# Nine one-unit slots for x, with joint loads in even periods and joint stores in odd ones, in a two-stage depthwise convolution

## The reference, cut to what matters

```python
def _L0_conv_ref(x, w1, w3, w5, alpha):      # depthwise, "same" padding
    return alpha[0]*x + alpha[1]*dw(x, w1) + alpha[2]*dw(x, w3) + alpha[3]*dw(x, w5)

def _L1_conv_ref(x, w, b):                   # one 3 x 3 kernel for all channels
    return conv3x3(x, w) + b

def _gn(v, G=32, eps=1e-05):                 # 32 groups of 3 channels
    ...
    return (g - mean) / sqrt(var + eps)

x = x + _L0_conv_ref(_gn(x), w1, w3, w5, alpha)
x = x + _L1_conv_ref(_gn(x), w, b)
```

## Time and profile before

| | |
|---|---|
| median of 3 runs | 429.32 us (427.31 to 429.94) |
| the profiled execution, its own time | 432.64 us |
| its span (first to last instruction) | 430.8 us |
| mean granted TensorE clock | 0.903 of full speed |
| busy PE, DVE, ACT, POOL | 318.5, 318.1, 304.1, 262.3 us |
| HBM read and written | 41.10 and 27.48 MB |

### The profile page before, as it was taken

How to read it: one execution, slowest core, us unless ns; L and a number is a source line. 1 busy time by engine, 2 the same in 40 slices (tenths; PEclk the granted TensorE clock), 3 DMA queues, 4 the chain that set the end, 5 groups by cost and what they waited for, 6 DMA issues and landing times.

```text
span 430.8 us, 12547 instructions
## 1 busy us (share of the span) xinstructions
PE 318.5 (74%) x5206; PEld 276.8 (64%) x5206; DVE 318.1 (74%) x688; ACT 304.1 (71%) x372; POOL 262.3 (61%) x206
## 2 busy tenths in 40 slices
PE   2491586754986998679894998499848989898440
PEld 2361273643986798459883897389836989897220
DVE  7861899971886998399929994889649996779620
ACT  1407257089999699939995899759993999977320
POOL 6405055058788578827885588738882788865601
PEclk9997596995999899969996999889998999999685
DMA  6689488201687769676986788676868514731965
GB/s 151 169 174 204 129 188 169 73 3 41 159 200 164 199 177 210 158 189 202 199 194 171 198 184 202 161 214 173 189 163 223 145 41 118 201 97 28 264 173 146
DMA packets 112829, 69.40 MB, mean 161 GB/s; under 512 B 4540, under 2 KB 109892, under 8 KB 112772
## 3 DMA queue, kind: packets, MB, share of 16 engines
q1 hardware_dynamic: 106088, 65.31, 60.5%
q10 hardware_dynamic: 6684, 3.29, 3.3%
HBM read 41.10 MB, written 27.48 MB: 159 GB/s over the span
## 4 chain that ended last, share of the span: by engine, by line
DVE 33%; DMA 21%; SPq 13%; ACT 13%; PE 9%; issue 4%; ACTq 2%; POOL 2%; POOLq 0%; DVEq 0%
DVE xt L697 15%; DVE stats L641 13%; DMA xt<-in_x_dram 10%; PE ps L377 8%; DMA edge_scratch<-gnX 6%; ACT gn_f L551 5%; SPq L236 5%; ACT gnX L552 4%; ACT cross L561 3%; SPq L216 3%; DMA edge_scratch<-gnY 2%; SPq L250 2%; POOL gnX L864 1%; SPq L263 1%; ACTq L244 1%
## 5 line engine op out<-in xcount | busy, mean ns | idle before, releaser
L377 PE MATMUL ps<-gnX,band 64*64 64x512 f16 x2880 | 181.6, 397 | 29.9 <-DVE xt L697 18.1
L377 PEld LDWEIGHTS ps<-gnX,band 64*64 64x64 f16 x2880 | 161.1, 188 | 46.6 <-issue 40.2
L697 DVE SCALAR_TENSOR_TENSOR xt<-ps,unscale,xt 128x512 f32<-128x512 f32 (+1 forms) x194 | 143.8, 747 | 22.9 <-PE ps L377 20.1
L641 DVE BATCH_NORM_STATS2 stats<-xt 128x6 f32<-128x384 f32 x256 | 120.9, 546 | 45.6 <-DMA xt<-in_x_dram 44.9
L377 PE MATMUL ps<-gnY,band 64*64 64x512 f16 x1728 | 116.8, 414 | 33.7 <-DVE xt L697 33.7
L864 POOL TENSOR_TENSOR gnX<-gn_f,gnX 128x768 f16<-128x768 f32 x60 | 92.7, 1545 | 60.7 <-ACT gnX L552 60.7
L377 PEld LDWEIGHTS ps<-gnY,band 64*64 64x64 f16 x1728 | 97.9, 190 | 49.1 <-ACT gnY L552 23.0
L551 ACT ACTIVATE gn_f<-xt,g_add,g_mul 128x768 f32<-128x768 f32 x120 | 122.1, 1017 | 4.9 <-DVE g_add L681 4.3
L864 POOL TENSOR_TENSOR gnY<-gn_f,gnY 128x768 f16<-128x768 f32 x60 | 92.7, 1545 | 31.0 <-ACT gnY L552 31.0
L561 ACT ACTIVATE cross<-ps,unscale 64x512 f32<-64x512 f32 x94 | 64.2, 683 | 51.0 <-PE ps L377 49.4
L873 POOL TENSOR_TENSOR xt<-xt,cross 128x512 f32<-128x512 f32 x47 | 61.7, 1315 | 57.3 <-ACT cross L561 57.2
(11 more groups left out here) (78 smaller groups left out, 97.9 us busy)
## 6 DMA issues: line engine op xcount, KB each, us to landing
out_dram<-xt SPq DMA_DIRECT2D x56, 384.0 KB, 4.8
xt<-in_x_dram SPq DMA_DIRECT2D x48, 384.0 KB, 6.4
band<-diag_scratch SPq DMA_DIRECT2D x48, 160.0 KB, 3.0
haloX<-edge_scratch SPq DMA_DIRECT2D x32, 123.4 KB
xt<-in_x_dram SPq DMA_DIRECT2D x20, 192.0 KB, 4.3
xt<-in_x_dram ACTq DMA_DIRECT2D x12, 192.0 KB, 6.0
out_dram<-xt SPq DMA_DIRECT2D x12, 192.0 KB, 4.0
haloX<-edge_scratch SPq DMA_DIRECT2D x32, 61.7 KB
```

Source lines behind the costliest of these rows:

```text
L377: mm = nc.tensor.matmul(ps[to, c, half, :], weights(rows, half), moving(rows, half), start=first, stop=last)
L641: st = nc.vector.bn_stats(stats[:, q_of(at, i) % 2, at, b, e, :], flat[:, SUB * e:SUB * (e + 1)])
L697: ev = nc.vector.scalar_tensor_tensor(out=here, in0=ps[frm, c, half, :].rearrange("h (b w) -> h b w", b=NB), scalar=unscale[rows, at:at + ...
```

## The change

The nine slots of `xt` hold one unit each (unit n in slot n % 9), and the two groups of a unit come from the two halves of the channels (unit n has channels 3n and 48 + 3n onwards). `PRE` = 4 units are loaded as before; the loads of units 4 and 5 stay in SP's period 1, and units j + 4 and j + 5 are loaded in even period j (2 to 10). Stores: unit 0 alone in period 3, then units j - 4 and j - 3 in odd period j (5 to 15), then units 13, 14 and 15 one by one. A pair whose slots lie side by side is one DMA per batch and half (384 KB); units 8 and 9 (slots 8 and 0) are loaded by two (192 KB each). Loads of a batch wait for the stores of that batch alone. To make room, `cross` has two buffers in turn in place of three, and `halo_wX` overlaps its blocks (pitch 66 in place of 128 columns). SP's order of border rows, bands and bulk within a period is as before.

```diff
-    NX = 4
+    NX = 9
+    PRE = 4
...
-        halo_w = [sb("halo_wX", [P, NU * CG, 2, R], fp16), sb("halo_wY", [P, 2, R], fp16)]
+        halo_w = [sb("halo_wX", [P, NU * CG * (R + FAR[0]) + R - FAR[0]], fp16), sb("halo_wY", [P, 2, R], fp16)]
...
-        xt = sb("xt", [P, NX, NB, 2, CG, 2, W])
+        xt = sb("xt", [P, NB, NX, CG, 2, W])
...
-        cross = sb("cross", [P, NCROSS, NB, W])
+        cross = sb("cross", [P, 2, NB, W])
...
         def first_channel(i, g):
-            return 4 * CG * (i // 2) + 2 * CG * g + CG * (i % 2)
+            return C // 2 * g + CG * i
...
+        def rows_of(n, g, b, units):
+
+            at = n % NX
+            return xt[HALVES[g], b, at:at + units, :, :, :].rearrange("p u c e w -> p (u c e) w")
+
+        def joint(n):
+
+            return n % NX + 1 < NX
...
+        def load(eng, n, b, units, done):
             for g in range(2):
...
+                eng.dma_start(rows_of(n, g, b, units), images(x, n, g, b, units)).then_inc(done, 16)
+
+        def store(eng, n, b, units):
             for g in range(2):
...
+                eng.dma_start(images(out, n, g, b, units), rows_of(n, g, b, units)).then_inc(stored[b], 16)
...
+            def stores_in(j):
+
+                if j < LAG + 1:
+                    return None
+                if j == LAG + 1 or j >= NU:
+                    return j - LAG - 1, 1
+                return (j - LAG - 2, 2) if j % 2 else None
+
+            def loads_in(j):
+
+                if j == 1:
+                    return PRE
+                return j + PRE if j % 2 == 0 and 2 <= j < NU - PRE else None
...
             def in_and_out(j, batches):
 
-                m = (j + 3) // 2 if j % 2 else j // 2 - LAG
                 for b in batches:
-                    if j % 2 and 2 <= m < NU // 2:
-                        if m >= NX:
-                            sp.wait_ge(stored[m % NX], 128 * (m // NX))
-                        load_pair(sp, m, b)
-                    elif j % 2 == 0 and m >= 0:
-                        unit_ready(2 * m + 1)
-                        store_pair(sp, m, b)
-                    elif j == PERIODS - 1:
-                        unit_ready(LAST - 1)
-                        store_unit(sp, LAST - 1, b)
+                    if stores_in(j) is not None:
+                        n, units = stores_in(j)
+                        unit_ready(n + units - 1)
+                        store(sp, n, b, units)
+                    n = loads_in(j)
+                    if n is not None:
+                        if n + 1 >= NX:
+                            sp.wait_ge(stored[b], 32 * stores_until(n + 1 - NX))
+                        if joint(n):
+                            load(sp, n, b, 2, x_in[n // 2 % 2])
+                        else:
+                            for k in range(n, n + 2):
+                                load(sp, k, b, 1, x_in[n // 2 % 2])
...
             def cross_over(i, c):
...
-                if i >= 1:
-                    act.wait_ge(cross_added, NCROSS * (i - 1) + min(c, NCROSS - 1) + 1)
+                k = crosses_before(i, c)
+                if k >= 2:
+                    act.wait_ge(cross_added, k - 1)
...
-            nc.vector.memset(halo_w[X][:, :, :, :], 0.0).then_inc(halo_w_zero, 1)
+            nc.vector.memset(halo_w[X][:, :], 0.0).then_inc(halo_w_zero, 1)
```

More of the change, by code:

```diff
@@ L133, in preact_conv_stack @@
         x_unit_in = [sem(f"x_unit_in{n}") for n in range(1, 4)]
-        x_in = [sem(f"x_in{r}") for r in range(NX)]
+        x_in = [sem(f"x_in{r}") for r in range(2)]
         band_in = [sem(f"band_in{p}") for p in range(2)]
-        stored = [sem(f"stored{r}") for r in range(NX)]
+        stored = [sem(f"stored{b}") for b in range(NB)]
         edges_landed = [sem(f"edges_landed{s}") for s in "XY"]
@@ L193, in crossed_to, with crosses_before @@
             return sum(crossed(n, c) for n in range(i + 1) for c in range(CG))
+        def crosses_before(i, c):
+            return crossed_to(i - 1) + sum(crossed(i, k) for k in range(c))
         def halo_landed(n):
@@ L239, in edges_in, with images, loaded @@
                        .then_inc(halo_in[s][p], 16)
-        def load_unit(eng, n, b, done):
+        def images(t, n, g, b, units):
+            c = first_channel(n, g)
+            return t[b, c:c + units * CG, :, :].rearrange("c (e p) w -> p (c e) w", e=2)
+        def rows_of(n, g, b, units):
[3 more added lines that the diff above has]
+            return n % NX + 1 < NX
+        def loaded(n):
+            return sum(128 if joint(k) else 256 for k in range(PRE, n + 1, 2) if (k - n) % 4 == 0)
+        def load(eng, n, b, units, done):
             for g in range(2):
[L243 to L247, removed]
+                eng.dma_start(rows_of(n, g, b, units), images(x, n, g, b, units)).then_inc(done, 16)
+        def store(eng, n, b, units):
             for g in range(2):
[L249 to L265, removed]
+                eng.dma_start(images(out, n, g, b, units), rows_of(n, g, b, units)).then_inc(stored[b], 16)
         @block.sync
@@ L276, in _ @@
             for b in range(2, NB):
-                load_unit(sp, 0, b, x_first_in[b])
+                load(sp, 0, b, 1, x_first_in[b])
             def save_runs(rows, to, done):
@@ L311, in _ @@
             for b in range(NB):
-                load_unit(sp, 1, b, x_unit_in[0])
+                load(sp, 1, b, 1, x_unit_in[0])
             edges_out(sp, X, 0)
@@ L323, in _ @@
             for b in range(NB):
-                load_unit(sp, 3, b, x_unit_in[2])
+                load(sp, 3, b, 1, x_unit_in[2])
             def unit_ready(n):
@@ L364, in _ @@
             for b in (0, 1):
-                store_unit(sp, LAST, b)
-            for r in range(NX):
-                sp.wait_ge(stored[r], 256 if r < NX - 1 else 384)
+                store(sp, LAST, b, 1)
+            for b in range(NB):
+                sp.wait_ge(stored[b], 32 * (stores_until(LAST) + 1))
         @block.tensor
@@ L523, in _ @@
             for b in range(2):
-                load_unit(act, 0, b, x_first_in[b])
+                load(act, 0, b, 1, x_first_in[b])
             act.wait_ge(const_ready, 3)
@@ L571, in halo_weights @@
                 for q in range(4):
[L572 removed]
+                    at = (R, R + 1, R - 2, R - 1)[q]
+                    nc.scalar.copy(halo_w[X][:, at:at + (R + FAR[X]) * (NU * CG - 1) + 1:R + FAR[X]], made[:, 0:NU * CG, q])\
                       .then_inc(halo_w_ready, 1)
@@ L582, in _ @@
             for b in range(NB):
-                load_unit(act, 2, b, x_unit_in[1])
+                load(act, 2, b, 1, x_unit_in[1])
             root(1)
@@ L613, in _ @@
             for b in (2, 3):
-                store_unit(act, LAST, b)
+                store(act, LAST, b, 1)
         @block.vector
@@ L869, in cross_add @@
             def cross_add(i, c):
-                pool.wait_ge(cross_out, crossed_to(i - 1) + sum(crossed(i, k) for k in range(c + 1)))
+                k = crosses_before(i, c)
+                pool.wait_ge(cross_out, k + 1)
                 here = x_of(i)[:, :, c, 1, :]
-                nc.gpsimd.tensor_tensor(here, here, cross[:, c, :, :], ALU.add).then_inc(cross_added, 1)
+                nc.gpsimd.tensor_tensor(here, here, cross[:, k % 2, :, :], ALU.add).then_inc(cross_added, 1)
             mid = diag[:, R - 1 - PAD:R + PAD, :][:, ::-1, :]
```

15 lines of the change are left out of this document (8 added, 7 removed).

## The result

| | before | after |
|---|---|---|
| median of 4 runs | 428.31 us (426.46 to 429.94) | 446.66 us (444.65 to 450.53) |
| ratio, 95% interval | | 1.044 (1.035 to 1.053) |
| profiled execution, its own time | 432.64 us | 446.02 us |
| its span | 430.8 us | 444.2 us |

The changed kernel is 4.4% slower. The forecast was 424 us with a range to 432, so it missed on the other side of no change. (The execution profiled before took 432.64 us, 4.3 above its median; of spans, the loss is 444.2 - 430.8 = 13.4 us.)

A forecast was written before the change was run, and what follows sets the result against it. SP's DMA issue queue was taken to bound the middle; -4.3 us at unit 12, -1.0 at the start and 0 at the end sum to -5.3, giving 424 us on the median of 429.32, range 413 to 432.

The forecast's parts named there:

- What bounds the kernel: Mid-kernel, SP's queue stays a second loop, so earlier loads gain a 7.4 us phase, not DVE's 34.7 us wait.
- SP's rounds: Periods 4 to 11: load rounds 23.7 us, store rounds 22.9, period 4 25.0; period 12 begins at 315.0, 3.1 later.
- At nothing: Two cross buffers, slot strides and the halves' channels cost nothing; another address order bounded by 1 us either way per period.
- Period 4: SP's period with 16 loads instead of 8: starts at 127.27 as before and takes 25.0 us, between 23.8 and 29.
- `save_pair`: Moving the save adds 1.57 us to SP's load periods, taken as 23.7 in all; store periods lose 0.3.
- The start: The smaller halo_wX cuts its memset from 2.62 to 1.38 us ahead of DVE's first work: -1.0 (0 to -1.2).
- The end: Last stores and border rows Y from period 15 on: fewer late stores against some coming later, 0 (-2 to +3).
- Rival C: Slower: band, save_pair and loads in one period fill SP's queue; rounds of 24.9 us give 435 us; chance 0.10.
- Rivals A: SP's rounds shrink to the compute loop and the whole 34.7 us wait for x is gained: 396 us; chance 0.06.
- half-way: SP's periods 4 to 11 at 22.3 us each, 178 instead of 187.7 in all: 415 us; chance 0.12.
- B: Nothing gained: SP's rounds 0.5 us longer each, period 12 starts at 319: 428 to 430 us; chance 0.22.
- The rule weighed there: Skill text that DMA issuing time is usually small; the prediction sided with rows showing SP issuing in 184.5 of 207.8 us.

The follow-up runs named there:

- e5: The changed kernel with an unused 192-byte gap behind halo_wX, putting xt and the tensors behind it back to the old address remainders: 419.91 us, ratio 0.981.
- e17: e5 plus a memset of 1536 more elements behind halo_wX's, taking back the 1.2 us gained by the smaller halo_wX: 427.06 us, ratio 0.992.
- e1: The kernel before with the two halves' channels 48 channels (3 MiB) apart in DRAM, as in the changed kernel: 430.49 us, ratio 1.003.
- e2: The kernel before with xt laid out by batch first, as in the changed kernel: 430.18 us, ratio 1.000.
- e10: e5 with save_pair moved from the load periods to the store periods: 419.64 us, ratio 0.975 against the kernel before.
- e8: The kernel before with xt alone moved to 256 bytes past a multiple of 512: 429.95 us, ratio 1.002.
- e9: The kernel before with the smaller halo_wX and its shorter memset, a gap keeping every other tensor in place: 426.41 us, ratio 0.991.
- e11: The kernel before with one more wait: SP issues unit 3's loads only once unit 2's have landed: 428.56 us, ratio 1.002.
- e4: The changed kernel with save_pair moved from the load periods to the store periods: 441.65 us, ratio 1.027 against the kernel before.
- e13: e5 with e11's wait and save_pair in store periods 3 to 11, pair 2 staying in period 2: 413.58 us, ratio 0.964.

## Why the prediction was wrong, point by point

- **What bounds the kernel.** This was right. SP's queue, not DVE's wait for x, sets periods 4 to 11: in the changed kernel SP waits for no compute engine there. Reading 34.7 us of DVE's wait as 34.7 us to gain would have been wrong by more. The gain of loading early was indeed a phase of 7.4 us: X of unit 12 followed SP's period 12 by 2.50 us (2.5 forecast), by 2.63 in e5 and 2.83 in e17.
- **SP's rounds: the step that failed.** 187.7 us forecast, 204.2 measured. These 16.5 us and the 1.7 by which period 4 began late are the whole miss at unit 12, 335.71 against 317.5; with the start's 1.0 that didn't come and 0.5 less at the end they make the 18.7 us by which the span missed (444.2 against 430.8 - 5.3). The prediction says under "At nothing" that the slots' strides move no more bytes, and bounds any price of the address by 1 us a round, since no row prices another address. The price was 2 us a round: 16.0 us in eight (e5). It asked about strides within xt and channels in DRAM, which both cost nothing (e1, e2), and not about where xt begins. The cause stood in its own text: `halo_wX` has 3230 instead of 6144 elements, costed as a memset only. With xt at a multiple of 512 the same schedule takes 188.2 us (e5) and 189.7 us (e17). Of the 14.5 us between e17 and the changed kernel 10.5 are longer waits for border rows to land (20.3 to 30.8), and 4.0 are in the rest of the rounds.
- **Period 4** with its 16 small loads: 25.0 forecast, 24.9 measured (129.01 to 153.93). That agreement is luck: with slow packets the other load rounds took 25.2 us, not 23.7, so that the 1.3 us more for 16 loads didn't show. In e5 they did in part, 24.8 against 23.9. Its start, said to stay at 127.27, was 129.01 with the shifted xt, and 127.26 in e17.
- **`save_pair`.** I took +1.5 us in a load round and -0.3 in a store round. Measured from e5 to e10: load rounds -2.0 on average, store rounds +1.0. The direction holds, and each size was about half a us too small.
- **The start.** -1.0 forecast. In the changed kernel unit 2's statistics began 0.26 us earlier (42.56); ACT issued its loads no earlier than before (24.20, before 24.17), against 22.72 in e5, so with the shifted xt nothing was left of the shorter memset. Aligned, the statistics began 7.3 us earlier (35.52 in e5), and the time gained 6 to 7. This term was mis-sized six- or sevenfold: here a landing time behind other traffic wasn't shifted by the same amount as the issue.
- **The end.** 0 forecast, -2 to +3. From X of unit 12 to the end it is 430.8 - 321.76 = 109.0 us before, 108.5 after, 105.8 in e5 and 105.9 in e17: -3.1 when aligned, a little outside my bounds. The kernels with the old schedule and xt in place spread from 107.2 to 110.2 there (e1, e2, e8, e9, e11), so 1 to 2 us of that may be the execution's own. SP's starts from 12 on were not 19 to 21 apart, as forecast, but 17.5, 22.9, 16.6 and 16.4.
- **The sum, once aligned.** In e17, whose start is that of before, unit 12 gives 319.80 - 321.76 = -2.0 (rounds 2.0 longer than forecast, phase 0.3 longer) and the end -3.1, together -5.1 against the -4.3 + 0 of the prediction. By the medians it is -3.0 (427.06 against 430.02): the execution profiled before was a long one.
- **Rival C** gave 435 us from rounds of 24.9, and its sign, starts 25 us apart, came (25.5). But its mechanism (band, save and loads in one period) is the smaller part: moving the save took 8.6 us off the rounds and 5.0 off the time (e4), and 4.1 off the rounds once xt is aligned, with no gain in time that can be told (e10), while the address took 16.0 off the rounds and 26.8 off the time with the save in its place (e5). Its number was nearer than its reason. Rivals A, half-way and B didn't happen.
- **Two cross buffers**, put at nothing: ACT's `cross_over` waited for PE alone in the changed kernel (63.1 us), never for POOL's add.
- **The rule weighed there**, that issuing time is usually small: SP waits for compute 0 us in periods 4 to 11 after, 1.1 in e5, so the rows' side was right.

## What to carry to other kernels

When a diff changes the size of any tensor, compare the start addresses of all DMA'd tensors behind it, before reasoning on the schedule; here 192 unused bytes were worth 27 us, more than the schedule. Keep a tensor that DMAs move in rows of 512 bytes, as here, at a multiple of 256 bytes; other row lengths were not tried. If one queue issues everything, a wait that an engine has for its data may be worth only the phase between that engine and the queue (7.4 of 34.7 us here), and the queue's round is the thing to shorten. Moving an issue from a full round into one that waits anyway took 4.1 us off eight rounds (e10); together with the wait for unit 2 the kernel then gained 6.3 us over e5 (e13).

## What the runs showed of the hardware that was not expected

- A packet of 512 bytes costs more when its SBUF side begins 64, 128, 192 or 320 bytes past a multiple of 512: 42.1 to 45.3 instead of 39.3 ns over all of q1, and 13 us (128 past) or 22 to 26 us (64, 192, 320 past) of 429 for this kernel, whose SP queue waits for landings. 256 past costs nothing that can be told (+0.7 us).
- The waits grow more than the packets' time: q1's busy time grows by 11% (260.6 to 288.7 us), SP's waits for landings in periods 4 to 11 by half, from 20.3 us (e17: 10.9 + 9.4) to 30.8.
- Loads issued 1.9 us earlier landed at least 9.3 us earlier (e9). The moment is not exact: issued alike, they landed 2.8 us apart in e5 and e10. But in the profiled executions that issued them at 22.25 to 22.74 us (e5, e9, e10, e13) the statistics began at 33.5 to 38.4, and in those that issued them at 23.9 to 25.2 (before, after, e1, e2, e4, e8, e11, e17) at 40.3 to 42.8.
- Whether 3 MiB or 384 KB lay between the two halves' channels in DRAM made no difference (e1, ratio 1.003, 0.999 to 1.006).
